# First attention of a two-block transformer kernel: one head per step, and a pair of heads per step

## The reference

```python
q = split_heads(x @ Wq.T); k = split_heads(x @ Wk.T); v = split_heads(x @ Wv.T)
sim = jnp.einsum('bhsd,bhtd->bhst', q, k) * scale
sim = jnp.where(causal[None, None], sim, -jnp.inf)
weights = jax.nn.softmax(sim, axis=-1)
out = jnp.einsum('bhst,bhtd->bhsd', weights, v)
out = out.transpose(0, 2, 1, 3).reshape(B, S, D_MODEL) @ Wo.T
...
x = x + _layernorm(_L0_attn_ref(_layernorm(x), Wq, Wk, Wv, Wo))
x = x + _layernorm(_L0_ffn_ref(_layernorm(x), ...))
```

## Time and profile before

| | us |
|---|---|
| median of 3 runs | 1419.59 (1417.71 to 1421.4) |
| the profiled execution | 1434.26 |
| its span | 1432.5 |
| TensorE busy | 1306.9 (91%) |
| TensorE weight loads busy | 1125.4 (79%) |
| VectorE busy | 1022.8 (71%) |
| ScalarE busy | 894.2 (62%) |
| GpSimd busy | 528.8 (37%) |

### The profile page before, as it was taken

How to read it: one execution, slowest core, us unless ns; L and a number is a source line. 1 busy time by engine, 2 the same in 40 slices (tenths; PEclk the granted TensorE clock), 3 DMA queues, 4 the chain that set the end, 5 groups by cost and what they waited for, 6 DMA issues and landing times.

```text
span 1432.5 us, 27089 instructions
## 1 busy us (share of the span) xinstructions
PE 1306.9 (91%) x7836; PEld 1125.4 (79%) x7836; DVE 1022.8 (71%) x3118; ACT 894.2 (62%) x2433; POOL 528.8 (37%) x868
## 2 busy tenths in 40 slices
PE   5999989989989989999999999999998878999940
PEld 4766766667669979999999899998997757999930
DVE  6588888978956757677877678667876655555536
ACT  3577766767757668776786767876676542444422
POOL 1300230412333344354364424734335251444434
PEclk9999999999999999999999999999999998999975
DMA  9993000000011331101122111211021333333353
GB/s 333 335 335 103 2 1 2 1 0 1 1 32 51 99 105 60 60 31 60 49 86 74 53 38 60 86 64 60 30 72 48 109 101 98 117 119 120 116 200 134
DMA packets 83615, 123.38 MB, mean 86 GB/s; under 512 B 7476, under 2 KB 68148, under 8 KB 83220
## 3 DMA queue, kind: packets, MB, share of 16 engines
q1 hardware_dynamic: 76612, 102.83, 22.5%
q0 software_dynamic: 6864, 18.88, 3.6%
HBM read 66.50 MB, written 55.18 MB: 85 GB/s over the span
## 4 chain that ended last, share of the span: by engine, by line
PE 71%; DVE 12%; issue 5%; ACT 4%; POOL 3%; DMA 2%; SPq 2%; another core or an unknown queue 1%; POOLq 0%; DVEq 0%; ACTq 0%
PE bank L1462 45%; PE bank L1567 8%; PE bank L1823 5%; PE bank L1641 4%; PE bank L1555 3%; DVE bank L1092 3%; PE bank L1545 3%; PE bank L1802 1%; PE bank L1833 1%; DVE hs L1313 1%; ACT p L928 1%; DMA yl<-ys_rows 1%; SPq L383 1%; DVE pT L1300 1%
## 5 line engine op out<-in xcount | busy, mean ns | idle before, releaser
L1092 DVE CUSTOM_DVE_ANT_0 bank<-bank,mask 128x512 f32<-128x512 f32 (+3 forms) x512 | 238.8, 518 | 36.3 <-PE bank L1545 18.3
L919 ACT ACTIVATE p<-bank,stat 128x512 f32<-128x512 f32 (+3 forms) x256 | 131.5, 526 | 133.3 <-DVE stat L1092 133.2
L1567 PE MATMUL bank<-pT,v_pad 128*128 128x128 f32 (+3 forms) x512 | 181.6, 457 | 17.3 <-DVE pT L1146 17.2
L1462 PE MATMUL bank<-xT,w_hl 128*128 128x512 f32 x768 | 190.2, 397 | 3.5 <-DVE hs L1313 3.0
L1462 PEld LDWEIGHTS bank<-xT,w_hl 128*128 128x128 f32 x768 | 145.4, 190 | 38.0 <-issue 3.5
L466 POOL CAST w_hl<-raw_qkv 128x512 fp32r<-128x512 f32 x96 | 58.9, 614 | 312.2 <-DMA raw_qkv<-in_qkvo 163.2
L816 ACT ACTIVATE p<-bank,stat 128x512 f32<-128x512 f32 (+3 forms) x256 | 133.0, 530 | 57.9 <-DVE stat L1092 57.9
L1462 PE MATMUL bank<-pT,v 128*128 128x128 f32 (+3 forms) x768 | 137.0, 327 | 0.0
L1462 PE MATMUL bank<-qk 128*128 128x512 f32 (+3 forms) x768 | 131.1, 320 | 3.0 <-DVE pT L1300 2.6
L928 ACT ACTIVATE p<-p,stat 128x512 f32<-128x512 f32 (+3 forms) x256 | 123.1, 552 | 15.2 <-DVE stat L1316 14.7
L1462 PEld LDWEIGHTS bank<-qk 128*128 128x128 f32 x768 | 120.6, 191 | 12.1 <-DVE v L1294 2.8
(11 more groups left out here) (243 smaller groups left out, 2886.5 us busy)
## 6 DMA issues: line engine op xcount, KB each, us to landing
xs_rows<-blank SPq DMA_DIRECT2D x1, 33410.0 KB, 115.1
raw_qkv<-in_qkvo SPq DMA_DIRECT2D x32, 768.0 KB
xrow<-xs_rows SPq DMA_DIRECT2D x79, 130.0 KB, 2.1
raw_o<-in_qkvo SPq DMA_DIRECT2D x32, 256.0 KB
yl<-ys_rows SPq DMA_DIRECT2D x16, 512.0 KB, 9.4
w_raw<-in_moe SPq DMA_DIRECT2D x12, 320.0 KB, 5.0
x_sb<-in_x SPq DMA_DIRECT2D x4, 512.0 KB, 6.6
out<-x_sb SPq DMA_DIRECT2D x4, 512.0 KB, 3.0
```

Of the source, the lines that this page charges most:

```text
L919: act.activation(p2[:, n % 2, POFF[qi]:POFF[qi + 1]], s2(t), ACT.Exp, scale=-1.0, bias=stat2[:, 0, n % 2, t:t + 1], accum_out=stat2[:, 1, ...
L1092: return dve.tensor_tensor_reduce(scores, scores, mask[:, TB - scores.shape[1]:], scale=-1.0, scalar=-2.0 * MASKED, op0=ALU.add, op1=ALU.m ...
L1462: ins = pe.matmul(out, a, b, start=start and i == 0, stop=stop and i == len(pairs) - 1, **kw)
L1567: pe.matmul(bank[O1_BANK][:, P * kj:TB], v1_pad[:, kj, prev, :], pT1[:, QOFF[kj]:QOFF[kj + 1]], start=(prev == 0 and t == 0), stop=(prev = ...
```

## The change

The first attention goes in steps of one pair of heads, 32 in all, and each score is computed twice. Scores by query (`score`, a query on each partition) serve only for the row minimum, which VectorE takes into `least`. TensorE turns the minima of both heads in one go (four transposes), and ScalarE copies them as two rows of one partition into row 0 and row 64 of the stack `stk`, whose other side holds ones. Scores by key (`score_t`, a key on each partition) then have the maximum already subtracted, their exponentials need no turning, and go in five full banks of 512 columns without a row sum; GpSimd zeroes what lies after the diagonal (`clear_future`). A column of ones beside the 16 value columns gives the sum. Four heads, each with 32 of the 128 weight columns, add in one bank; ScalarE copies it out, TensorE turns it, VectorE divides by the sum (`weigh`), TensorE turns it back, ScalarE copies it to `oT1`. The stacks are no longer products with `sel` but 14 DMA transfers per pair into one of four slots, issued by SyncE (`load_stack`), and the fill of `xs_rows` is cut into 32 pieces between them (`prefill`). The scaling of the four tiles between the batches is all on ScalarE. The loops are written out, in place of a hardware loop.

```diff
+        ITEMS = {4: (0, 1), 3: (3, 4), 2: (2, 2), 1: (3, 4)}
+        S1_PARTS, S1_REST = ((0, 4), (1, 4), (0, 2)), ((0, 3), (1, 3), (0, 1), (1, 1))
+        N1 = B * H1 // 2
+        O1_BANK, FREE_BANK = 6, 7
...
+            first = 3 * P if n == 1 else 0
+            return bank[2 if n == 2 else a][:, first:first + P * n]
+        def st1(s, i):
+            return bank[3 + (5 * s + i) % 3]
...
+            def load_stack(s):
...
+                if s >= NSTK:
+                    sp.wait_ge(a1_st, 6 * (s - NSTK + 1))
+                for w, src, part, row in ((0, q1_hl, HI, 1), (0, q1_hl, LO, 2), (0, q1_hl, HI, 3),
+                                          (1, k1_hl, HI, 1), (1, k1_hl, HI, 2), (1, k1_hl, LO, 3)):
+                    for a in range(2):
+                        to = slice(64 * a + DH1 * row, 64 * a + DH1 * (row + 1))
+                        sp.dma_start(f32(stk[to, slot, w, :]),
+                                     f32(src[first + DH1 * a:first + DH1 * (a + 1), g, part, :])).then_inc(stk_in[slot], 16)
+                for a in range(2):
+                    sp.dma_start(f32(stk[64 * a:64 * a + 1, slot, 0, :]), f32(stk[64 * a + 1:64 * a + 2, slot, 0, :]))\
+                      .then_inc(stk_in[slot], 16)
...
+            sp.wait_ge(stk_zero, 3)
+            sp.wait_ge(ph1_lo, 4)
+            for s in range(NSTK):
+                load_stack(s)
...
+            for s in range(N1):
+                if s >= NSTK:
+                    load_stack(s)
+                prefill(s)
...
+            def clear_future(s):
...
+                for part, taken in zip(diagonals, (2, 3, 4, 5)):
+                    pool.wait_ge(a1_exp, 5 * s + taken)
+                    pool.affine_select(out=part, in_=part, compare_op=ALU.is_ge, fill=0.0, base=0,
+                                       pattern=[[0, 2], [1, P]], channel_multiplier=-1).then_inc(a1_sel, 1)
...
+            def step1(s):
+                fill_v(s)
+                clear_future(s)
+                b, k = s // (N1 // B) - 1, s % (N1 // B)
+                if s == 0:
+                    split_qk(0)
+                if s == 1:
+                    split_v()
+                if s == 2:
+                    split_qk(1)
+                if s == 3:
+                    split_o()
+                if b >= 0 and k == 2:
+                    norm_y(b)
+                if b >= 0 and k == 4:
+                    make_x1(b)
+                if b >= 0 and k == 5:
+                    norm_x1(b)
...
+            def step1(s):
+                b, k = s // (N1 // B) - 1, s % (N1 // B)
+                def exp(i):
+                    act.wait_ge(a1_st, 6 * s + (i + 1 if i < 2 else i + 2))
+                    if i == 0 and s >= 2:
+                        act.wait_ge(a1_pv, s - 1)
+                    act.activation(pT1[:, s % 2, i, :], st1(s, i)[:, :], ACT.Exp).then_inc(a1_exp, 1)
+                if s < N1:
+                    act.wait_ge(a1_mt, s + 1)
+                    for a in range(2):
+                        act.activation(stk[64 * a:64 * a + 1, s % NSTK, 0, :], free[64 * a:64 * a + 1, :], ACT.Copy)\
+                           .then_inc(a1_m, 1)
+                if b >= 0 and k == 2:
+                    take_y(b, 0, free)
+                if b >= 1 and k == 0:
+                    take_xT(b - 1, 0, free)
+                if s < N1:
+                    for i in range(3):
+                        exp(i)
+                if s >= 2 and s % 2 == 0:
+                    act.wait_ge(a1_pv, s)
+                    act.wait_ge(a1_ot, s // 2 - 1)
+                    act.activation(o1_sum[:, :], bank[O1_BANK][:, :], ACT.Copy).then_inc(a1_oe, 1)
+                if s >= 5 and s % 4 == 1:
+                    g = (s - 5) // 4
+                    act.wait_ge(a1_xt, g + 1)
+                    if g >= 2:
+                        act.wait_ge(m_y, 2 * (g // 2))
+                    act.activation(oT1[:, g % 2, :], free[:, :], ACT.Copy).then_inc(a1_o, 1)
+                if b >= 0 and k == 2:
+                    take_y(b, 1, free)
+                if b >= 0 and k == 4:
+                    scale_u(b)
+                if b >= 0 and k == 7:
+                    scale_xn(b)
+                if b >= 1 and k == 0:
+                    take_xT(b - 1, 1, free)
+                if s < N1:
+                    for i in range(3, 5):
+                        exp(i)
+                if b >= 1 and k in (0, 1):
+                    scale_hs(b - 1, k)
...
+                def weigh(i):
+                    dve.wait_ge(a1_ot, i + 1)
+                    heads = free[:, :].rearrange("p (j h n) -> p j h n", j=TPB, h=4)
+                    dve.reciprocal(o1_rec[:, :, :].unsqueeze(3), heads[:, :, :, DH1:DH1 + 1]).then_inc(a1_rec, 1)
+                    dve.wait_ge(a1_rec, i + 1)
+                    own = o1[:, :, 4 * DH1 * (i % 4):4 * DH1 * (i % 4 + 1)].rearrange("p j (h n) -> p j h n", h=4)
+                    dve.tensor_tensor(own, heads[:, :, :, 0:DH1],
+                                      o1_rec[:, :, :].unsqueeze(3).to_broadcast([P, TPB, 4, DH1]), ALU.mult)\
+                        .then_inc(a1_xo, 1)
...
+                def score(r, a, n):
+                    rows, m, qi = slice(64 * a, 64 * a + 64), r % NSTK, n - 1
+                    return pe.matmul(s1(a, n), stk[rows, m, 0, P * qi:P * (qi + 1)], stk[rows, m, 1, 0:P * n],
+                                     start=True, stop=True)
+                def score_t(a, n):
+                    rows, m, kj = slice(64 * a, 64 * a + 64), s % NSTK, TPB - n
+                    i, first = item(a, n)
+                    return pe.matmul(st1(s, i)[:, first:first + P * n], stk[rows, m, 1, P * kj:P * (kj + 1)],
+                                     stk[rows, m, 0, P * kj:TB], start=True, stop=True)
+                def value(r, a, n):
+                    kj, first, last = TPB - n, (r % 2, a, n) == (0, 0, TPB), (r % 2, a, n) == (1, 1, 1)
+                    return pe.matmul(bank[O1_BANK][:, P * kj:TB], v1_pad[:, r % 2, kj, a, :],
+                                     pt1(r, a, n), start=first, stop=last, skip_group_check=True)
+                r = s + 1
+                if r < N1:
+                    pe.wait_ge(stk_in[r % NSTK], 16 * 14 * (r // NSTK + 1))
+                    for i, (a, n) in enumerate(S1_PARTS):
+                        if r >= 1:
+                            pe.wait_ge(a1_max, 6 * (r - 1) + i + 4)
+                        score(r, a, n).then_inc(a1_s, 1)
+                if 0 <= s < N1:
...
+                    pe.wait_ge(a1_max, 6 * (s + 1))
+                    turn(lambda j: least[:, s % 2, j, :], a1_mt, free)
+                if 1 <= s <= N1:
+                    if s % 2 == 1 and s >= 3:
+                        pe.wait_ge(a1_oe, s // 2)
+                    pe.wait_ge(a1_vpad, 2 * s)
+                    pe.wait_ge(a1_sel, 4 * (s - 1) + 1)
+                    for a in range(2):
+                        value(s - 1, a, TPB)
+                if 0 <= s < N1:
+                    pe.wait_ge(a1_m, 2 * (s + 1))
+                if s >= 3 and s % 2 == 1:
...
+                    turn(lambda j: o1_sum[:, P * j:P * (j + 1)], a1_ot, free)
+                if b >= 0 and k == 2:
+                    pe.wait_ge(a1_o, 2 * (b + 1))
+                    project_y(0, free)
...
+                if r < N1:
+                    for a, n in S1_REST:
+                        if n == 3:
+                            pe.wait_ge(a1_max, 6 * r + 1 + a)
+                        ins = score(r, a, n)
+                        if n == 1:
+                            ins.then_inc(a1_s, 1)
+                    pe.wait_ge(a1_max, 6 * r + 3)
+                    score(r, 1, 2).then_inc(a1_s, 1)
+                if 0 <= s < N1:
+                    for i, (a, n) in enumerate(S1_PARTS):
+                        if s >= 1:
+                            pe.wait_ge(a1_exp, 5 * (s - 1) + i + 3)
+                        score_t(a, n).then_inc(a1_st, 1)
+                if 1 <= s <= N1:
+                    pe.wait_ge(a1_sel, 4 * s)
+                    for n in range(TPB - 1, 0, -1):
+                        for a in range(2):
+                            ins = value(s - 1, a, n)
+                    ins.then_inc(a1_pv, 1)
+                if s >= 5 and s % 4 == 1:
+                    g = (s - 5) // 4
+                    pe.wait_ge(a1_xo, 2 * g + 2)
+                    turn(lambda j: o1[:, j, P * (g % 2):P * (g % 2 + 1)], a1_xt, free)
+                if b >= 0 and k == 2:
+                    pe.wait_ge(m_ys, 2 * b + 1)
+                    project_y(1, free)
...
+                if 0 <= s < N1:
+                    pe.wait_ge(a1_st, 6 * s + 3)
+                    score_t(1, 2).then_inc(a1_st, 1)
+                    for a, n in S1_REST:
+                        if n == 3:
+                            pe.wait_ge(a1_exp, 5 * s + 1 + a)
+                        ins = score_t(a, n)
+                        if n == 1:
```

(54 more changed lines are left out.)

539 lines of the change are left out of this document (182 added, 357 removed).

## The result

The changed kernel is slower by 1%. Its median is 1434.1 us (1432.8 to 1436.1, four runs) against 1419.9 for the kernel before (1417.7 to 1421.4, four runs): the ratio is 1.0102, with a 95% interval of 1.0085 to 1.0120. The forecast was 1412 and faster; the time lies within the range of 1372 to 1440, on the side that was given 0.31.

What follows compares the result with a forecast made beforehand. TensorE was taken to bound the first attention: start to 68.6, 31 steps of 8.9 (276), boundaries 40, end 12, giving 397.4 against 405.65; less 1 in the second attention, 7 us saved: 1412 us, range 1372 to 1440.

Steps and rivals of the forecast that it cites:

- the side that was given 0.31: Whole kernel: the outcome that the change makes it slower than the kernel before, chance 0.31.
- The queue of SyncE: First attention, each pair: 15 issues at 0.40 to 0.50 us, 6.0 to 7.5 us, fit inside a step of 8.9.
- The rival: SyncE's issues set the first attention's step from 0.60 us each; at 0.88 the time is near 1465; chance 0.04.
- just hidden: Before attention: 56 issues take 22 to 28 us, within some 28 us before the projection's end at 56.
- step 1: First attention's start: after memsets, first minima, copies and exponentials, this step begins 12.4 us after 56.2, at 68.6.
- As hidden in 32 pieces: Prefill of 33.4 MB, moved out of the projections into the first attention, stays hidden when cut up; no cost.
- The price of small transfers: Stack transfers of 32 KB or less: the rule against small transfers adds time only if the queue is the bound.
- TensorE's work: First attention, per pair: 8.65 us of TensorE issue against 9.29 before, including 3.12 for scores and 4.64 for values.
- The overlap: First attention's scores in different row groups run at once: 1.2 us less per pair, 1376 us; chance 0.18.
- The ScalarE loop: First attention: stack-row copies and exponentials make TensorE wait 0.25 us per pair; as slower rival 0.86, 1431 us, chance 0.26.
- Boundaries: Between batches of the first attention: 13.7 us each against 8.7 now, 40 us against 26 over three.
- What follows the last step: End of the first attention: last values, sums, weighing and output take 12 us, 0.8 more for the meeting.

Runs made afterwards that it cites:

- The late fill: The changed kernel with 14 transfers, all 32 pieces of the fill behind the last stack transfer on SyncE's queue; 1465.3 us, ratio 1.021.

## Why the prediction was wrong

**The queue of SyncE: the step that failed.** It said 15 issues at 0.40 to 0.50 us, 6.0 to 7.5 inside a step of 8.9. They cost 10.84: 14 at 0.62, 0.58 for the piece and 1.37 for the hold behind it, with 0.04 between groups. So the queue was the bound and not hidden, and TensorE waited for it in 25 of 31 steps. The rival was there, with the right threshold (0.60 us per issue; it was 0.72), and was given 0.04. The earlier trace rows had two prices, 0.40 and 0.88, both of loads from DRAM, and I took the lower as the nearest in size. Size was not what decides here: the queue run by itself shows 0.62 within SBUF from one row to 128. The fairer reading was that no row showed the kind, so either price could hold, and at the middle of the two, 0.64, the queue already binds. The range should have leant there.

**The same price at the start.** The 56 issues were "just hidden" at 22 to 28 us; they took 36.6. The prediction put step 1 at 68.6; its turn came at 81.0, so the step began at about 80, 11.4 late. Of that 7.9 is the wait for SyncE at the meeting: first scores at 66.79, against 58.94 with seven transfers. Another 2.7 is the later end of the projections, which the prediction put at nothing. It had weighed the memset of the stack's slots against the identity alone, and left out the two memsets of ones behind it, 3.65 us together, beside which VectorE's small instructions are slow.

**"As hidden in 32 pieces."** The piece cost 1.95 us of the queue per step, its own issue and the hold, though no engine waited for its bytes. The late fill shows it: 8.84 per round without it.

**The price of small transfers.** The Trainium skill, DMA: Bandwidth & Descriptors, Bandwidth, says that transfers under 64 KB are dominated by their descriptors and advises larger batches. The prediction set that aside by the spacing of 0.40. The runs are on the side of the advice: seven transfers, six of 64 KB, in place of fourteen of 32 KB or less are worth 0.04 of the kernel's time (0.970 against 1.010). They do not show its reason: within SBUF 2 KB in one row and 256 KB in 128 rows cost the queue the same, so what counted here was the number of issues.

**TensorE's work was over-estimated.** Eight scores take 0.84 and not 1.56, in both groups. By the prediction's other terms (values 4.64, transposes 0.4) that gives 6.7 for a plain step; 6.8 was measured with seven transfers, values at 4.6. The overlap, a rival at 0.18, is real, and halving the scores by it was right to a tenth. The Trainium skill, TensorE: Matmul & The Clock Gate, Part 3, says that matmuls in different row groups run at once; the traces agree (0.84 against 1.47 us). The changed kernel shows none of this gain in its time, because the queue covers it.

**The ScalarE loop.** The one-row copy at 0.55 (measured 0.59) and the exponential at 0.58 (0.60 long, starts 0.49 apart) were well sized. It binds only at boundaries: steps of 11.1 to 13.5 us with both copies on ScalarE fall to 9.1 and 10.2 without. The steps with the output projection (11.5 to 12.2) hardly change, so something else binds those. Boundaries were forecast at 13.7 each over plain steps. With seven transfers, 31 steps take 272.6 us against 226 at the mean of 6.8 and 7.8; of the difference of 46 some 3 stand ahead of the first boundary, so the three cost some 14 each, as forecast. In the changed kernel they cost next to nothing of their own, as four slots of lead and a step of 11 cover them.

**Why the total was still near.** By luck: two errors cancelled. 31 steps were to take 276 and boundaries 40, together 316; from about 80 to 403.2 they took 323. The 25 steps of 11.0 are 2.1 longer than forecast each, 53 us; the boundaries' 40 do not come on top, and the other six steps are 6 shorter. The end is 18 us late (projection at 415.88, forecast 397.4): 11 from the start and 7 from the steps. What follows the last step was right, 12.7 against 12.8.

## What to carry to other kernels

Count the issues of each queue per step and price them by kind (here about 0.6 us within SBUF, 0.39 to 0.53 from DRAM) before asking how many bytes they move; where the trace has no row of the kind, take both ends of what it has as equally likely. Small loads on a queue that also carries large writes can pay for both: here 1.95 us per step. And when a queue is the bound, first make its transfers fewer and wider: other savings, like the overlap of scores here, show only after that.

## What the runs showed that was not expected

- The issue of a transfer within SBUF took 0.622 to 0.639 us for 16 rows of 256 bytes and for 128 rows of 2 KB alike.
- A write of 1 MB to DRAM, eight times 1040 bytes from each partition, held up the transfers behind it on the same queue by 1.3 to 1.4 us.
- A wait shown for weight loads (0.76 us) cost nothing where a matmul of 512 columns was still running; read both of TensorE's rows before counting one.
- VectorE took 0.70 us to copy one row of 512 elements from PSUM, ScalarE 0.59.
- Two VectorE instructions on 128x4 elements took 1.60 and 1.62 us beside GpSimd's memsets of one row, and 0.16 without them.
